# Self attention of a decoder layer in one kernel: the order of TensorE's work within a quad of heads, and what ScalarE and VectorE do in between

## What is computed

```
Q = rope(x @ Wq.T + bq);  K = rope(x @ Wk.T + bk);  V = x @ Wv.T + bv      # 32 heads of 16
scores = Q @ K.T / sqrt(16), future keys at -inf
out = softmax(scores) @ V                                # per head
x = layernorm(x + out @ Wo.T + bo)
```

## Time and profile before

| | |
|---|---|
| median of 3 runs | 3002.29 us (3001.25 to 3004.66) |
| the profiled execution: its time | 2996.66 us |
| its span | 2994.6 us |
| TensorE (PE) busy | 2749.7 us, 92% of the span |
| VectorE (DVE) busy | 2039.7 us, 68% |
| ScalarE (ACT) busy | 1953.2 us, 65% |
| GpSimd (POOL) busy | 1646.9 us, 55% |
| mean granted TensorE clock | 0.967 of full speed |

### The profile page before, as it was taken

One profiled execution on the slowest core, in us unless ns is written; L12 is line 12 of the kernel. 1 busy time (PEld: TensorE's weight loads), 2 busy tenths in 40 slices (PEclk: granted clock), 3 DMA queues, 4 the chain that ended last, 5 costly groups with the idle time before them and its releaser, 6 DMA issues.

```text
span 2994.6 us, 60845 instructions
## 1 busy us (share of the span) xinstructions
PE 2749.7 (92%) x20784; PEld 2532.8 (85%) x20784; DVE 2039.7 (68%) x4012; ACT 1953.2 (65%) x4168; POOL 1646.9 (55%) x1678
## 2 busy tenths in 40 slices
PE   6799999998879999999888999999987899999996
...
GB/s 175 136 142 223 165 226 169 205 64 99 127 38 37 99 50 93 50 93 51 137 88 39 36 93 54 89 57 86 65 124 95 32 71 65 79 64 78 64 43 109
DMA packets 97920, 285.13 MB, mean 95 GB/s; under 512 B 9936, under 2 KB 18256, under 8 KB 94416
## 3 DMA queue, kind: packets, MB, share of 16 engines
...
## 4 chain that ended last, share of the span: by engine, by line
PE 67%; issue 10%; POOL 9%; ACT 6%; DVE 5%; DMA 2%; SPq 0%; DVEq 0%; ACTq 0%; POOLq 0%
PE bank L1053 38%; PE dn L1053 14%; PE sp L1053 10%; POOL kept_s L534 4%; ACT ph L731 2%; PE bank L1118 1%; PE sp L1195 1%; POOL orw L553 1%; PE sp L1203 1%; ACT pt L655 1%; POOL ol L557 1%; PE sp L1282 1%; ACT sp L736 1%; DVE mcol L933 1%; DMA wqk<-in_ws 1%
## 5 line engine op out<-in xcount | busy, mean ns | idle before, releaser
L534 POOL TENSOR_TENSOR kept_s<-kept_s,mrow 128x512 f32<-128x512 f32 (+1 forms) x896 | 1061.9, 1214 | 595.1 <-ACT mrow L721 594.9
L944 DVE TENSOR_TENSOR pl<-sp,ph 128x512 fp32r<-128x512 f32 (+1 forms) x896 | 577.9, 645 | 79.5 <-ACT sp L736 76.2
L731 ACT ACTIVATE ph<-kept_s 128x512 fp32r<-128x512 f32 (+1 forms) x896 | 534.0, 596 | 43.8 <-POOL kept_s L534 41.7
L736 ACT ACTIVATE sp<-kept_s 128x512 f32<-128x512 f32 (+1 forms) x896 | 506.2, 565 | 2.4 <-DVE sua L952 2.4
L1053 PE MATMUL dn<-ph,vh 128*128 128x256 f32 (+1 forms) x1664 | 489.7, 294 | 2.2 <-DVE pl L944 1.3
L1053 PE MATMUL dn<-ph,vl 128*128 128x256 f32 (+1 forms) x1664 | 471.8, 284 | 0.0
L1053 PE MATMUL dn<-pl,vh 128*128 128x256 f32 (+1 forms) x1664 | 471.1, 283 | 0.0
L952 DVE TENSOR_TENSOR sua<-sp,sua 128x512 f32<-128x512 f32 (+1 forms) x640 | 401.2, 627 | 0.0
L713 ACT ACTIVATE kept_s<-bank 128x512 f32<-128x512 f32 x384 | 228.5, 595 | 232.7 <-PE bank L1053 232.2
L713 ACT ACTIVATE kept_s<-sp 128x512 f32<-128x512 f32 x384 | 228.6, 595 | 191.1 <-PE sp L1053 190.7
L1053 PEld LDWEIGHTS dn<-ph,vh 128*128 128x128 f32 (+1 forms) x1664 | 316.8, 190 | 10.3 <-DVE pl L944 3.1
...
## 6 DMA issues: line engine op xcount, KB each, us to landing
wqx<-wq SPq DMA_DIRECT2D x128, 512.0 KB, 3.3
...
```

The costliest lines, as they stand in the source:

```text
L534: nc.gpsimd.tensor_tensor(kept_s[:, n % 2, i:z, :], kept_s[:, n % 2, i:z, :], mrow[:, n % 2, :].unsqueeze(1).broadcast_to([P, z - i, S]), ...
L731: nc.scalar.activation(ph[:, k % PH, 0:cols], src, ACT.Exp, scale=XSCALE).then_inc(ph_ok, 1)
L736: nc.scalar.activation(pbank[k % 2][:, 0:cols], src, ACT.Exp, scale=XSCALE).then_inc(pr_ok, 1)
L944: nc.vector.tensor_tensor(pl[:, k % PH, 0:cols], src, ph[:, k % PH, 0:cols], ALU.subtract).then_inc(pl_ok, 1)
```

## The change

Nothing is computed otherwise; instructions are placed in another order, and pt gets a second half. In turn u of TensorE's loop there are now the four transposes of quad u itself, `score_quad(u + 1)` between its heads 2 and 3, the projections cut into pieces of one to four calls, `weigh_quad` cut into its two key blocks (the second goes behind the next quad's first transposes), and the first two calls of the next q projection at the end of the odd turns. The ninth turn is gone. ScalarE does exponentials two heads ahead of the copies, and the two context pieces of a quad at its end. VectorE does all maxima of a quad first, then either the division (even u) or the whole turning (odd u). Of the output projection, the calls of blocks 0 to 2 of both row tiles come before the wait for the last block.

```diff
--- before.py
+++ after.py
@@ -245,7 +245,7 @@
             vx = sb("vx", [P, 2, TB, HB, 2 * DH], stack=st)
             oe = sb("oe", [P, 2, 2 * DH], stack=st)
             pn = sb("pn", [P, PNR, 384], stack=st)
-            pt = sb("pt", [P, QH4, 384], stack=st)
+            pt = sb("pt", [P, 2 * QH4, 384], stack=st)
             nmx = sb("nmx", [P, PNR, 2], stack=st)
             rcs = sb("rcs", [P, S], stack=st)
             otn = sb("otn", [P, S], stack=st)
@@ -650,31 +650,39 @@
 
                     n = (b * NQ + u) * QH4 + j
                     act.wait_ge(s_tp, n + 1)
-                    if b * NQ + u:
-                        act.wait_ge(s_pvq, b * NQ + u)
-                    nc.scalar.activation(pt[:, j, :], s_turn[:, 0:3 * P], ACT.Copy).then_inc(s_ptc, 1)
+                    if b * NQ + u >= 2:
+                        act.wait_ge(s_pvq, b * NQ + u - 1)
+                    nc.scalar.activation(pt[:, n % (2 * QH4), :], s_turn[:, 0:3 * P], ACT.Copy).then_inc(s_ptc, 1)
+
+                def take_context(u, i):
+
+                    mc, k = divmod(2 * u + i, len(CTX_PIECES))
+                    r = raw_at(b, mc, 2 * k if b == 0 else k)
+                    a, z = CTX_PIECES[k]
+                    act.wait_ge(raw_ld[r % 2], 16 * (r // 2 + 1))
+                    high_part(ctxh[:, mc, a:z], raw[:, r % 2, 0:z - a])
 
                 take_qk(0)
                 take_v(0)
-                for u in range(NQ + 1):
+                for u in range(NQ):
                     m, e = divmod(u, 2)
-                    for j in range(QH4):
-                        if u:
-                            take_turned(u - 1, j)
-                        if u < NQ:
-                            quad_exps(u, j)
-                        if e and m and j == 1:
-                            take_heads(m - 1)
-                        if m + 1 < NM and e == 0 and j == 2:
+                    quad_exps(u, 0)
+                    quad_exps(u, 1)
+                    take_turned(u, 0)
+                    quad_exps(u, 2)
+                    take_turned(u, 1)
+                    quad_exps(u, 3)
+                    take_turned(u, 2)
+                    take_context(u, 0)
+                    take_turned(u, 3)
+                    if m + 1 < NM:
+                        if e == 0:
                             take_qk(m + 1)
-                        if m + 1 < NM and e and j == 3:
+                        else:
                             take_v(m + 1)
-                        if u < NQ and j % 2:
-                            mc, k = divmod(2 * u + j // 2, len(CTX_PIECES))
-                            r = raw_at(b, mc, 2 * k if b == 0 else k)
-                            a, z = CTX_PIECES[k]
-                            act.wait_ge(raw_ld[r % 2], 16 * (r // 2 + 1))
-                            high_part(ctxh[:, mc, a:z], raw[:, r % 2, 0:z - a])
+                    take_context(u, 1)
+                    if e == 0 and m:
+                        take_heads(m - 1)
                 take_heads(NM - 1)
 
                 def job_high(kind, p, i):
@@ -862,19 +870,16 @@
                 mask_queries(0)
                 for u in range(NQ):
                     m, e = divmod(u, 2)
-                    if e and m:
-                        divide_heads(m - 1)
                     for j in range(QH4):
                         quad_maxima(u, j)
-                        if m + 1 < NM:
-                            if e == 0 and j == 3:
-                                turn_products(m + 1, 0)
-                            elif e and j == 1:
-                                turn_products(m + 1, 1)
-                                turn_sum(m + 1, 0)
-                            elif e and j == 2:
-                                turn_sum(m + 1, 1)
-                                mask_queries(m + 1)
+                    if e == 0 and m:
+                        divide_heads(m - 1)
+                    elif e and m + 1 < NM:
+                        turn_products(m + 1, 0)
+                        turn_products(m + 1, 1)
+                        turn_sum(m + 1, 0)
+                        turn_sum(m + 1, 1)
+                        mask_queries(m + 1)
                 divide_heads(NM - 1)
                 dve.wait_ge(bias_ok, at(b, 2 * TB, TB))
                 for tb in range(TB):
@@ -1063,16 +1068,17 @@
                 pe.wait_ge(xt_ld, at(b, 16, 16))
                 pe.wait_ge(f_res, at(b, TB, 0))
 
-                def project_qk(m, kind):
+                def project_qk(m, kind, chunks):
 
                     t = b * NM + m
                     if kind == 0:
                         pe.wait_ge(wqk_ld, at(t, 16, 16))
                         pe.wait_ge(s_v, 4 * t)
-                    for c in range(DC):
+                    for c in chunks:
                         last = mm(pj[:, kind * S:(kind + 1) * S], wqk[:, kind * D + c * P:kind * D + (c + 1) * P], xt[:, c, :],
                                   c == 0, c == DC - 1)
-                    last.then_inc(s_qk, 1)
+                    if c == DC - 1:
+                        last.then_inc(s_qk, 1)
 
                 def swap_pairs(m):
 
@@ -1081,16 +1087,16 @@
                     for kind in range(2):
                         mm(pj[:, kind * S:(kind + 1) * S], swap[:, :], qkb[:, kind, :], True, True).then_inc(s_sw, 1)
 
-                def project_v(m):
+                def project_v(m, tb):
 
                     t = b * NM + m
                     pe.wait_ge(wv_ld, at(t, 16, 16))
                     pe.wait_ge(s_rope, at(t, N_ROPE, 4))
-                    for tb in range(TB):
-                        for c in range(DC):
-                            last = mm(pj[:, tb * P:(tb + 1) * P], xt[:, c, tb * P:(tb + 1) * P], wv[:, c * P:(c + 1) * P],
-                                      c == 0, c == DC - 1)
-                    last.then_inc(s_vp, 1)
+                    for c in range(DC):
+                        last = mm(pj[:, tb * P:(tb + 1) * P], xt[:, c, tb * P:(tb + 1) * P], wv[:, c * P:(c + 1) * P],
+                                  c == 0, c == DC - 1)
+                    if tb == TB - 1:
+                        last.then_inc(s_vp, 1)
 
                 def score_quad(u):
 
@@ -1118,49 +1124,68 @@
                         last = nc.tensor.transpose(s_turn[:, z:z + P], pn[:, n % PNR, a:a + P], ident)
                     last.then_inc(s_tp, 1)
 
-                def weigh_quad(u):
+                def weigh_quad(u, kb):
 
                     t, e = b * NM + u // 2, u % 2
-                    pe.wait_ge(s_ptc, (b * NQ + u + 1) * QH4)
-                    pe.wait_ge(s_v, 4 * (t + 1))
-                    if e == 0:
-                        pe.wait_ge(s_fin, 2 * t)
-                    for kb, a, z, w in ((0, 0, 0, S), (1, S, P, P)):
-                        for part in range(2):
-                            for j in range(QH4):
-                                out_rows, i = slice(32 * j, 32 * (j + 1)), e * QH4 + j
-                                last = mm((s_den if part else dn)[out_rows, z:z + w], oe[:, e, :] if part else vx[:, t % 2, kb, i, :],
-                                          pt[:, j, a:a + w], e == 0 and kb == 0, e == 1 and kb == 1)
-                    last.then_inc(s_pvq, 1)
+                    a, z, w = ((0, 0, S), (S, P, P))[kb]
+                    if kb == 0:
+                        pe.wait_ge(s_ptc, (b * NQ + u + 1) * QH4)
+                        pe.wait_ge(s_v, 4 * (t + 1))
+                        if e == 0:
+                            pe.wait_ge(s_fin, 2 * t)
+                    for part in range(2):
+                        for j in range(QH4):
+                            out_rows, i = slice(32 * j, 32 * (j + 1)), e * QH4 + j
+                            last = mm((s_den if part else dn)[out_rows, z:z + w], oe[:, e, :] if part else vx[:, t % 2, kb, i, :],
+                                      pt[:, (b * NQ + u) % 2 * QH4 + j, a:a + w], e == 0 and kb == 0, e == 1 and kb == 1)
+                    if kb == 1:
+                        last.then_inc(s_pvq, 1)
+
+                def output_part(tb, m):
+
+                    return mm(mx[:, tb, :], ots[:, m, tb * P:(tb + 1) * P], wos[:, m, 0:D], m == 0, m == NM - 1)
 
                 for kind in range(2):
-                    project_qk(0, kind)
+                    project_qk(0, kind, range(DC))
                 swap_pairs(0)
-                project_v(0)
-                for u in range(NQ + 1):
+                for tb in range(TB):
+                    project_v(0, tb)
+                score_quad(0)
+                project_qk(1, 0, (0, 1))
+                for u in range(NQ):
                     m, e = divmod(u, 2)
+                    ahead = m + 1 < NM
+                    turn_head(u, 0)
                     if u:
-                        turn_head(u - 1, 0)
-                    if u < NQ:
-                        score_quad(u)
-                    for j in range(QH4):
-                        if u and j:
```

(43 more changed lines are left out.)

## The result

| | before | changed |
|---|---|---|
| median of 4 runs | 3002.85 us (3001.25 to 3004.66) | 2935.77 us (2929.37 to 2938.22) |
| ratio of the runs, 95% interval | | 0.9773 (0.9756 to 0.979) |
| the profiled execution: time, span | 2996.66, 2994.6 us | 2936.57, 2934.8 us |
| TensorE (PE) busy | 2749.7 us, 92% | 2736.7 us, 93% |
| mean granted clock | 0.967 | 0.976 |

The change takes 67 us off the median and 60 off the profiled execution. The forecast was 2942 us, in a range of 2925 to 2971.

A forecast was written before the change was run, and what follows sets the result against it. The self attention stages were taken to be bound by handovers between engines, turn b = 0 by SP's queue. Stage gains -16.4 - 18.9 - 16.5 - 8.3, say -60, from 3002.3 gave 2942 us, range 2925 to 2971.

The forecast's parts named there:

- odd turn, even turn: Steady quads, scores to next scores: 7.8 and 8.65 us, a pair 16.4 against 18.65; head 3's exponentials end last in even turns.
- quad 7's scores to the division, full clock: End of the stage, to the last division: three links of 1.19 us and the weighing, 10.2 us against 17.3.
- division to the first key product: Output part: six of eight calls run during division and bias add, 7.6 us against 12.2.
- half clock in the end: Last weighing and first output calls at 1.2 GHz: 1.1 weighing, 0.7 longer links, 1.7 output calls, 3.5 us a stage.
- Rival 3: Steady quads: scores don't come earlier, pairs stay at 18.65 us, only the end gains: -36, 2966 us; chance 0.1.
- Scores early, pt in two halves: In the quads: scores come earlier; pt's second half removes no wait that ends last, but the late weighing block needs it.
- the five terms: Stage of b = 1 without the clock's 3.5 us: 14.3 + 2 x 16.4 + 7.5 + 10.2 + 7.6.
- Rival 1: End of each stage: the clock holds at 2.4 GHz, -73, 2929 us; chance 0.15.
- b = 0: First turn, bound by SP's queue: -1.7 + 1.6 + 0.7 - 6.0 - 2.9 = -8.3 us.
- wqk for b > 0: Later turns: needed 3.5 us behind the even quad's scores, issued about 2.5 before, landing at 2.1 with 4.6 us.
- Rivals 2 and 4: Early calls wait for wqk: 4 us late, -30, 2972 us, chance 0.12; 10 us each, +20, 3022 us, chance 0.03.
- the sign that the forecast called wrong: In turns b > 0: `DMA wqk` as PE's releaser would show the forecast wrong; no size given.

The follow-up runs named there:

- e5_exps_ahead: Changed kernel with ScalarE doing the next quad's head 0 exponentials ahead of the read of q/k or v: 2927.41 us, ratio 0.9747.
- e8: Changed kernel with the next quad's scores behind head 3's transposes instead of in front of them: 2942.18 us, ratio 0.9806.
- e10: Changed kernel with both key blocks weighed ahead of the next quad's first transposes and pt back to one half: 2945.63 us, ratio 0.9795.
- e9: Changed kernel with both key blocks weighed ahead of the next quad's first transposes, pt keeping both halves: 2937.21 us, ratio 0.9775.
- e1: Changed kernel with all eight output products behind the wait for the last block again: 2955.52 us, ratio 0.9834.
- e0_after: Control: the changed kernel, unedited, profiled and timed again: 2933.23 us, ratio 0.9771 to the kernel before.

## Why the prediction was right, point by point

| term, b = 1 | forecast | measured |
|---|---|---|
| quad 0's to quad 2's scores | 14.3 | 14.24 |
| odd turn, even turn | 7.8, 8.65 | 7.83, 8.57 |
| quad 6's to quad 7's scores | 7.5 | 7.43 |
| quad 7's scores to the division, full clock | 10.2 | 10.12 (b = 2) |
| division to the first key product | 7.6 | 7.77 |
| half clock in the end | 1.1 + 0.7 + 1.7 = 3.5 | 1.05 + 0.25 + 0 = 1.3, 0, 1.3 (b = 1, 2, 3) |
| stage, less before | -16.4, -18.9, -16.5 | -18.66, -22.50, -18.74 |

**The steady quads.** Right, link by link. From the scores of the even turn, the forecast had the swap at 4.15, the next transposes at 5.65 and 6.85 and the scores at 8.65; the rows above give 4.09, 5.53, 6.75 and 8.57. That head 3's exponentials and not PE end last there is shown twice: by ScalarE's unbroken row of work, and by `e5_exps_ahead`, where 0.54 us goes when one of its pieces moves. In odd turns PE ends last, and the same edit on ScalarE leaves 7.83 as it is. The odd turn came out link by link too: the q calls at 3.63, the transposes at 4.59 and 5.76 and the scores at 7.83, for 3.45, 4.5, 5.65 and 7.8. Rival 3, a ring that holds pairs at 18.65, is out.

**Scores early, pt in two halves.** Both as argued: the scores alone are worth 0.7 to 0.9 us a quad, 1.19 in the first (`e8`), the second half of pt nothing without the late block (the stages of `e10` against those of `e9`).

**The end.** At full clock the five terms make 72.4, and the stage of b = 2, which never left 1.00, took 72.37. The step that failed is the clock: I let the last weighing and the first products be at 1.2 GHz in every stage, 3.5 us each: 1.1 for the weighing, 0.7 for longer links, 1.7 for the products. Here are, in the changed kernel's timeline, the last transposes and weighing of b = 1 (from 844) and of b = 2 (from 1561):

```profile
844.16 0.52 PE L1124 MATMUL bank<-cst,pn 128*128 128x128 f32 x3 [0.67 <-ACT pt L655]
845.36 0.77 PE L1124 MATMUL bank<-cst,pn 128*128 128x128 f32 x3 [0.67 <-ACT pt L655]
846.71 1.08 PE L1058 MATMUL dn<-pt,vx 128*32 128x256 f32 x8 [0.58 <-ACT pt L655]
...
1561.25 0.52 PE L1124 MATMUL bank<-cst,pn 128*128 128x128 f32 x3 [0.67 <-ACT pt L655]
1562.44 0.52 PE L1124 MATMUL bank<-cst,pn 128*128 128x128 f32 x3 [0.67 <-ACT pt L655]
1563.54 0.64 PE L1058 MATMUL dn<-pt,vx 128*32 128x256 f32 x8 [0.58 <-ACT pt L655]
```

With the same holes, 0.67, 0.67 and 0.58 us, the lower level came in one and not in the other. Where it came, the window from 837.92 to 849.35 has a granted clock of 0.85, which is 3.4 us of its 11.43 at the lower level, and it cost 1.3: the links 0.25 (1.35 from 845.36 to 846.71, for 1.10 in b = 2) and the weighing 1.05 (2.49 to the products at 849.20, for 1.44). The products ran at 2.4 GHz in all three later stages (7.14). The 1.7 for them was taken from the 8.61 of before, but those stood behind a wait of 2.88 that the early products remove; `e1`, with the wait put back, has the slow products again (8.81). 10.5 us in three stages were charged and 2.6 spent. That is the 8 us by which these three stages beat the sum. Rival 1 (the clock holds) was true of one stage in three. By the Trainium skill (TensorE: Matmul & The Clock Gate, Part 1) activity releases the throttle and the level is one of two; the rows agree with the two levels, but show that here the holes' length alone does not say which one is granted.

**b = 0.** Forecast -8.3, measured -7.81. Its chain is SyncE's, through wqk. The rows behind the pair that the earlier trace rows show before, ScalarE's piece, SyncE's issue, and the projection:

```profile
55.07 0.53 ACT L603 ACTIVATE ctxh<-raw 128x400 fp32r<-128x400 f32 x1
...
69.45 0.38 SPq L411 DMA_DIRECT2D wqk<-in_ws  x1
...
74.12 2.08 PE L1058 MATMUL bank<-xt,wqk 128*128 128x256 f32 x4 [6.66 <-DMA wqk<-in_ws]
```

The pair's scores are at 54.58 and 79.77. The piece starts 0.49 behind them, 19.05 later the projection starts, and 5.65 later come the next scores: 25.19, against 0.6 + 19.3 + 5.7 = 25.6 and 24.04 before. The projection starts 19.54 us behind the pair's scores for 14.02 before, as the piece that starts the chain stands 5.74 us later against them, and PE's wait grew from 3.71 to 6.66 us. The other parts: up to quad 3's scores -1.7 as forecast (-0.5 to quad 1's, -1.2 from there), the pair +1.15 for 1.6, quads 5 to 7 +0.97 for 0.7, from quad 7's scores on -8.24 for -8.9. How close these come is in part luck: in `e0_after` the same pair takes 27.14 us and the stage 101.89, a gain of 5.7 for the 8.3.

**wqk for b > 0.** Needed 3.6 us behind the even quad's scores, for 3.5 forecast, issued 1.9 and 2.5 us before them for 2.5, and no row of the later blocks names its DMA. Only the projection of the turn's second block, in front of quad 0's transposes, a call that the forecast didn't cost, waits, for 0.36, 0.25 and 0.30 us in b = 1, 2 and 3. So the sign that the forecast called wrong, `DMA wqk` as PE's releaser in b > 0, did show once a stage, and costs next to nothing. Rivals 2 and 4 are out. Issue to use is 3.98 and 4.67 us in b = 0 and 4.60 at that projection in b = 1. These are near the 4.6 that I took from rows. The estimate of 3.2 by the Trainium skill (DMA: Bandwidth & Descriptors, Anatomy of one DMA) is below all three; that section states its fit for transfers issued from GpSimd, and wqk is issued by SyncE, so the figure need not hold for it.

**The sum.** The stages made -67.7 for -60.1. The profiled execution gained just 60.1, because 7.9 us more passed outside the stages in it than in the profile of before; the medians, 67.1 apart, agree with the stages. So the -60 that the two profiles show is no proof of the sum: two misses cancel, the clock's 8 us and the rest of the program's 8. Against the median of the changed kernel the forecast was 6 us too high; the clock term, 8 us too large in the stages, is of that size. The stages of b = 1 to 3 came out at 82.44, 81.14 and 82.44 us, just below the 83 to 86 that were to show the forecast right, for the same reason.
